# Mixture logits: the bias in the place of the last feature

## The chip, the cores and the metric

The kernel runs on one core of a Trainium2 chip. The metric is the time of one execution on the device in microseconds; a run gives one time, and the median of several is compared. Engines are named as in the profile: PE is TensorE (PEld its weight loads), DVE is VectorE, ACT is ScalarE, POOL is GpSimd, and SP is SyncE, which here only issues DMA transfers.

## The reference

4,096 tokens of 256 features pass through attention, a mixture layer, a second attention and the same mixture layer again, each on the layer-normed input and added to it. This is the mixture layer (n = 64 experts of p = 32 slots, 2,048 slots in all):

```python
logits = (jnp.einsum('tzd,ed->tze', x, phi_w) + phi_b).reshape(t, z, n, p)
D = jax.nn.softmax(logits, axis=3)
C = jax.nn.softmax(logits, axis=2)
X_tilde = jnp.einsum('tznp,tzd->npd', D, x)
...
X_tilde = jnp.tanh(X_tilde)
Y_tilde = jnp.einsum('npd,ndH->npH', X_tilde, expert_w) + expert_b[:, None, :]
Y = jnp.einsum('tznp,npH->tzH', C, Y_tilde)
```

The `x` of this function is a layer norm without weights: the 256 features of a token have mean zero, so the last one is minus the sum of the others.

## The kernel before

The program is a row of stages, one after the other, with a barrier of all engines between them (`phase_of`). Each engine has its instruction list for a stage, and semaphores order them inside it. The stages are: `load_and_cut`; then for each of the two halves (tags a and f, then b and g) a layer norm, the projections, attention and output projection, and for the mixture layer (f, g) a layer norm, `dispatch`, `experts` and `combine`.

**load_and_cut** (DVE, POOL, SP, a little PE; the first 43 us). SP loads phi transposed, two groups of 128 features by 2,048 slots. DVE finds the largest magnitude (a maximum and a minimum over everything, L96 and L97, then a transpose on PE to spread it over partitions), and cuts phi, scaled by a power of two, into a high and a low half of 16 bits (L123, L125), which SP stores in DRAM as `phi_parts` for both mixture layers. It does the same for the bias row, on one partition, in three bf16 parts (L221 to L229, `bparts`), stored as `pb_parts`. DVE's last work there is the scales of the attention weights (L217, L219, a gather on PE at L200, L233 to L245). POOL builds identity matrices and masks from tiles that DVE clears; SP copies two of them with their halves swapped (`mask_turned`, `identb_turned`) at the end of its list, behind the store of `pb_parts`.

**The layer norm of a mixture layer** writes the normed tokens scaled by 256, transposed (features on partitions), as a high and a low half: `xlnT[feature, part, c, token]`. While it runs, SP loads its list `loads`: phi's two parts, the bias parts `pb3`, and `pbcol`, the bias with slots on partitions.

**dispatch** works in 64 units: 32 tiles of 128 tokens for the first 1,024 slots, and the same for the others. For unit n, PE computes the logits into two PSUM banks: for each bank six matmuls (high x high, high x low, low x high, for two groups of features; L1002) and one with the bias (L1004), 3 rows of ones against the three bias parts. DVE takes the maxima over the slots of an expert (L1105) and over the experts (L1106, kept for combine), and subtracts the first (L1110). ACT exponentiates (L1042); DVE sums (L1094) and inverts (L1098), ACT scales the inverse (L1047), POOL multiplies (L1083), ACT casts to the high half (L1050), POOL makes the low half (L1087), and PE multiplies with the tokens, 24 matmuls into four accumulator banks (L1015). The lists are staggered:

```python
for n in range(UNITS_D + LAG):
    if n < UNITS_D:
        logits(n)
    if n >= LAG:
        products(n - LAG)
    if n in TURN_AFTER:
        turn(TURN_AFTER[n])
```

`LAG` is 3. On DVE, the sum and inverse of unit n-1 stand behind the subtraction of unit n; on ACT the exponential of n stands ahead of the scaling and the cast of n-1. The logits have two slots of two banks, so `logits(n)` waits for the subtraction of n-2. After 8 units of the second half (n = 39, 47, 55, 63) a chunk of maxima is combined on DVE (L1117) and cut in three by four small operations on POOL, between the multiplication and the low half of that unit; three units later PE transposes it (L1024) in one of the logits slots, and ACT copies it out behind its cast of that iteration. When the first half is through, ACT copies the four accumulators out (L1055), and the products of unit 32 wait for it.

**combine** computes the logits again, transposed, 16 blocks for each group of 512 tokens, with six matmuls (L1268) and one (L1272) that subtracts the kept maxima; the bias comes in as ACT's per-partition operand of the exponential (L1319).

Of the kernel before, what the change touches and what calls it, by code (L numbers as in the profile page):

```python
# [129 lines left out]
def load_and_cut(nc, m, ps, x_in, phi_in, pb_in, phi_parts, pb_parts, qk_weights):  # L130
# [3 lines left out]
    with phase_of(nc, "cut") as (ctx, sem, sb):  # L134
        phi, parts = sb("phi", [P, DC, SLOTS]), sb("parts", [P, 2, DC, SLOTS], F16)
        row, rest = sb("row", [1, SLOTS]), sb("rest", [1, SLOTS])
        bparts = sb("bparts", [1, 3, SLOTS], BF16)
# [66 lines left out]
        def _(dve):  # L204
# [19 lines left out]
            dve.wait_ge(row_cut, 2)  # L224
            dve.tensor_tensor(rest[:, :], row[:, :], bparts[:, 0, :], ALU.subtract).then_inc(row_cut, 1)
            dve.wait_ge(row_cut, 3)
            dve.tensor_copy(bparts[:, 1, :], rest[:, :]).then_inc(row_cut, 1)
# [1258 lines left out]
```

## Time and profile before

| | |
|---|---|
| median of 3 runs | 5185.71 us |
| lowest, highest | 5184.31, 5189.25 us |
| the profiled execution | 5181.14 us |
| its span, first to last instruction | 5179.4 us |
| mean granted clock of TensorE | 0.944 of full |
| PE busy | 4608.4 us (89%) |
| DVE busy | 4098.5 us (79%) |
| ACT busy | 3144.7 us (61%) |
| POOL busy | 1188.4 us (23%) |
| first dispatch stage, first to last matmul | 1688.5 to about 2104 us |
| second dispatch stage, first matmul | 4253.8 us |

The profile is of one execution, and its rows are times within that. Busy shares are means over stages with different limits; what an edit is worth is read from its own stage. A full clock is 1.00, which is 2.4 GHz; 0.50 is 1.2 GHz.

### The profile page before, as it was taken

To read this page: it belongs to the slowest core of one execution; us is meant where nothing else is said; L and a number is where in the kernel's file an instruction comes from. 1 tells how busy PE (TensorE), PEld (TensorE's weight loads), DVE (VectorE), ACT (ScalarE), POOL (GpSimd) and SP (SyncE) were. 2 spreads that over 40 slices of the span, in tenths; PEclk is the share of its full clock that TensorE was granted. 3 is DMA by queue.
4 is the path that set the end of the run, shared out by engine and by line. 5 is a ranking of instruction groups with operands and counts; after the bars stand their busy time and mean duration, and the time that the engine had idled before them with its cause. 6 is when DMAs were issued, how large, how long until landed. Compare 5 with 4: busy or idle time off the path is not lost. (4 is left out here: it accounts for less than half of the span.)

```text
span 5179.4 us, 97856 instructions
## 1 busy us (share of the span) xinstructions
PE 4608.4 (89%) x40558; PEld 2002.5 (39%) x40558; DVE 4098.5 (79%) x4682; ACT 3144.7 (61%) x5855; POOL 1188.4 (23%) x1174
## 2 busy tenths in 40 slices
PE   5589999999997999689867899999999979996998
PEld 2322223322234555355533222232222345552555
DVE  5399999999875778477745999999998768774776
ACT  1267898889995334234323789888899933332433
POOL 0000001100003567243300000011000126662342
PEclk9699999999998999799977999999999989997999
DMA  3100000000000000400021000000000000005000
GB/s 125 47 20 8 2 14 14 14 14 2 2 2 21 1 1 1 147 1 0 1 68 34 17 8 2 19 9 14 14 2 2 2 19 1 1 1 147 9 12 13
DMA packets 70480, 106.94 MB, mean 21 GB/s; under 512 B 9465, under 2 KB 57721, under 8 KB 65919
## 3 DMA queue, kind: packets, MB, share of 16 engines
q1 hardware_dynamic: 70064, 101.08, 6.1%
q8 instruction: 300, 4.92, 0.4%
q14 instruction: 116, 0.94, 0.1%
HBM read 76.73 MB, written 23.08 MB: 19 GB/s over the span
## 5 line engine op out<-in xcount | busy, mean ns | idle before, releaser
L871 DVE TENSOR_REDUCE b_att_mx<-ps 128x2 f32<-128x1024 f32 (+3 forms) x1152 | 1227.3, 1130 | 112.4 <-PE ps L724 71.6
L871 DVE TENSOR_REDUCE a_att_mx<-ps 128x2 f32<-128x1024 f32 (+3 forms) x1152 | 1227.3, 1130 | 110.7 <-PE ps L724 69.7
L828 ACT ACTIVATE a_att_pt<-ps 128x512 f32<-128x512 f32 (+3 forms) x2304 | 1149.5, 561 | 212.7 <-PE ps L760 180.6
L828 ACT ACTIVATE b_att_pt<-ps 128x512 f32<-128x512 f32 (+3 forms) x2304 | 1149.7, 561 | 211.3 <-PE ps L760 179.6
L779 PE MATMUL ps<-b_att_pt,b_v 128*17 128x256 f32 (+1 forms) x8704 | 671.3, 381 | 9.7 <-ACT b_att_osb L815 9.0
L779 PE MATMUL ps<-a_att_pt,a_v 128*17 128x256 f32 (+1 forms) x8704 | 671.2, 381 | 9.7 <-ACT a_att_osb L815 9.1
L760 PE MATMUL ps<-b_q,b_k 51*128 51x512 f16 (+3 forms) x1152 | 367.0, 369 | 0.3 <-ACT b_att_pt L828 0.2
L760 PE MATMUL ps<-a_q,a_k 51*128 51x512 f16 (+3 forms) x1152 | 366.9, 369 | 0.3 <-ACT a_att_pt L828 0.2
L760 PE MATMUL ps<-a_att_q,a_att_k 51*128 51x512 f16 (+3 forms) x1152 | 340.4, 365 | 1.0 <-ACT a_att_pt L828 0.7
L760 PE MATMUL ps<-b_att_q,b_att_k 51*128 51x512 f16 (+3 forms) x1152 | 339.9, 365 | 1.3 <-ACT b_att_pt L828 0.5
L705 POOL TENSOR_SCALAR_AFFINE_SELECT b_att_pt<-b_att_pt 128x512 f32<-128x512 f32 x128 | 81.4, 636 | 1126.8 <-ACT b_att_pt L828 1114.4
L705 POOL TENSOR_SCALAR_AFFINE_SELECT a_att_pt<-a_att_pt 128x512 f32<-128x512 f32 x128 | 81.3, 636 | 1125.8 <-ACT a_att_pt L828 1113.4
L724 PE MATMUL ps<-a_k,a_q 48*128 48x512 f16 (+3 forms) x1152 | 290.2, 380 | 36.3 <-DVE a_att_mx L871 32.8
L724 PE MATMUL ps<-b_att_k,b_att_q 48*128 48x512 f16 (+3 forms) x1152 | 318.7, 365 | 3.0 <-DVE b_att_mx L871 2.5
L724 PE MATMUL ps<-a_att_k,a_att_q 48*128 48x512 f16 (+3 forms) x1152 | 317.9, 365 | 3.0 <-DVE a_att_mx L871 2.5
L724 PE MATMUL ps<-b_k,b_q 48*128 48x512 f16 (+3 forms) x1152 | 289.5, 379 | 34.1 <-DVE b_att_mx L871 30.5
L779 PEld LDWEIGHTS ps<-a_att_pt,a_v 128*17 128x17 f32 x8704 | 145.5, 95 | 358.0 <-ACT a_att_pt L828 217.5
L779 PEld LDWEIGHTS ps<-b_att_pt,b_v 128*17 128x17 f32 x8704 | 145.6, 96 | 357.2 <-ACT b_att_pt L828 212.5
L1319 ACT ACTIVATE g_comb_ct<-ps,g_pbcol,unscale 128x512 f32<-128x512 f32 x128 | 99.3, 776 | 208.4 <-PE ps L1272 208.4
L1319 ACT ACTIVATE f_comb_ct<-ps,f_pbcol,unscale 128x512 f32<-128x512 f32 x128 | 99.3, 776 | 207.5 <-PE ps L1272 207.5
L1281 PE MATMUL ps<-f_comb_yp,f_comb_ct 128*128 128x256 f16 x1536 | 186.2, 282 | 38.2 <-DVE f_comb_ct L1366 38.2
L1281 PE MATMUL ps<-g_comb_yp,g_comb_ct 128*128 128x256 f16 x1536 | 186.3, 282 | 37.0 <-DVE g_comb_ct L1366 37.0
(309 smaller groups left out, 7652.5 us busy)
## 6 DMA issues: line engine op xcount, KB each, us to landing
f_exp_w<-in_expert_w SPq DMA_DIRECT2D x64, 256.0 KB, 5.8
g_exp_w<-in_expert_w SPq DMA_DIRECT2D x64, 256.0 KB, 5.4
x<-in_x SPq DMA_DIRECT2D x1, 4096.0 KB, 19.6
a_parts_q<-a_qkv_cut SPq DMA_DIRECT2D x16, 256.0 KB, 2.8
a_parts_k<-a_qkv_cut SPq DMA_DIRECT2D x16, 256.0 KB, 2.7
b_parts_q<-b_qkv_cut SPq DMA_DIRECT2D x16, 256.0 KB, 2.8
b_parts_k<-b_qkv_cut SPq DMA_DIRECT2D x16, 256.0 KB, 2.7
out<-x SPq DMA_DIRECT2D x8, 512.0 KB
```

The lines of the kernel that those rows point to most:

```text
L705: pool.affine_select(out=block_p, in_=block_p, pattern=[[0, 4], [1, P]], compare_op=ALU.is_ge, fill=0.0, base=0, channel_multiplier=-1).th ...
L724: mm = pe.matmul(ps[:, at:at + width], q[quad % 2][h // 2][r:r + ROWS, t0:t0 + P], k[quad % 2][h // 2][r:r + ROWS, c * BANK:c * BANK + wid ...
L760: pe.matmul(ps[:, at:at + width], k[quad % 2][h // 2][r:r + ROWS_M, kb * P:(kb + 1) * P], q[quad % 2][h // 2][r:r + ROWS_M, (g + 1) * BANK ...
L779: mm = pe.matmul(OUT[32 * h:32 * h + VW, lo:hi], v[:, kb, 4 * quad + h, :], pt[:, s % PT_RING, h, lo - left:hi - left], start=(first and h ...
L828: act.activation(pt[:, s % PT_RING, i, 0:width], ps[:, at:at + width], ACT.Exp, scale=unscale).then_inc(pt_ready, 1)
L871: dve.tensor_reduce(mx[u % 2][:, h:h + 2, t, c], both, AX.X, ALU.max).then_inc(ring_read, 1)
L1281: mm = pe.matmul(ps[:, (Y + zt) * BANK:(Y + zt) * BANK + D], ctp[1 - parity][:, kb, cp * BANK + zt * P:cp * BANK + (zt + 1) * P], yp[:, y, ...
L1319: act.activation(ct[parity][:, b, :], ps[:, (LT + b % 4) * BANK:(LT + b % 4 + 1) * BANK], ACT.Exp, bias=pbcol[:, b:b + 1], scale=m.unscale ...
```

## The change

The layer-normed features add up to zero, so a sum over 256 features with weights w is a sum over the first 255 with weights w minus the last weight. The place of the 256th is free: its row of phi holds the bias, divided by 2^15 / 256, and its row of `xlnT` the constant 2^15. The logits come out of the six matmuls with the bias in them; the bias matmul of dispatch, the bias parts and the bias operand of combine are gone. The subtraction is done once, on the chip, in `load_and_cut`.

```diff
@@ load_and_cut
-        row, rest = sb("row", [1, SLOTS]), sb("rest", [1, SLOTS])
-        bparts = sb("bparts", [1, 3, SLOTS], BF16)
+        last, col = sb("last", [P, SLOTS]), sb("col", [P, 1])
+        ones_row = sb("ones_row", [1, 2, N], F16)
...
-            sp.dma_start(row[:, :], pb_in.rearrange("(a s) -> a s", a=1)).then_inc(row_loaded, 16)
+            sp.dma_start(last[:, :], last_in.partition_broadcast(P)).then_inc(loaded, 16)
...
-            sp.wait_ge(row_cut, 6)
-            sp.dma_start(pb_parts, bparts[:, :, :]).then_inc(stored, 16)
-            sp.wait_ge(built, 1)
+            sp.wait_ge(row_made, 2)
+            sp.dma_start(x_rows, ones_row[:, :, :]).then_inc(stored, 16)
+            sp.wait_ge(built, 2)
...
+            pool.memset(ones_row[:, 0, :], X_ONE).then_inc(row_made, 1)
+            pool.memset(ones_row[:, 1, :], 0.0).then_inc(row_made, 1)
             pool.wait_ge(cleared, 1)
+            pool.affine_select(out=col[:, :], in_=col[:, :], pattern=[[0, 1]], compare_op=ALU.not_equal,
+                               fill=XLN_SCALE / X_ONE, base=1 - P, channel_multiplier=1).then_inc(built, 1)
+            pool.wait_ge(built, 1)
...
-            dve.memset(m.onesb[:, :], 1.0).then_inc(cleared, 1)
-            dve.wait_ge(loaded, 16)
+            dve.memset(col[:, :], 1.0).then_inc(cleared, 1)
+            dve.wait_ge(loaded, 32)
+            dve.tensor_tensor(phi[:, 0, :], phi[:, 0, :], last[:, :], ALU.subtract).then_inc(folded, 1)
+            dve.tensor_tensor(phi[0:P - 1, 1, :], phi[0:P - 1, 1, :], last[0:P - 1, :], ALU.subtract).then_inc(folded, 1)
+            dve.wait_ge(built, 1)
+            dve.wait_ge(folded, 2)
+            dve.tensor_scalar(phi[P - 32:P, 1, :], phi[P - 32:P, 1, :], col[P - 32:P, 0:1], None, ALU.mult).then_inc(folded, 1)
+            dve.wait_ge(folded, 3)
             n = scales.make(dve, phi_f, ps[:, 0:P], chain, gathered)
...
-            dve.wait_ge(row_loaded, 16)
-            dve.tensor_scalar(row[:, :], row[:, :], bscale[0:1, 0:1], None, ALU.mult).then_inc(row_cut, 1)
-            dve.wait_ge(row_cut, 1)
-            dve.tensor_copy(bparts[:, 0, :], row[:, :]).then_inc(row_cut, 1)
...
-            dve.tensor_tensor(bparts[:, 2, :], rest[:, :], bparts[:, 1, :], ALU.subtract).then_inc(row_cut, 2)
-            dve.wait_ge(row_cut, 6)
@@ layernorm
-            return xlnT[:, part, c, tg * BANK:(tg + 1) * BANK], ps[:, (i % 4) * BANK:(i % 4 + 1) * BANK]
+            rows = P - (c == DC - 1)
+            return xlnT[0:rows, part, c, tg * BANK:(tg + 1) * BANK], ps[0:rows, (i % 4) * BANK:(i % 4 + 1) * BANK]
@@ dispatch, logits(n)
-                        pe.matmul(ps[:, at:at + BANK], xlnT[:, xp, c, t * P:(t + 1) * P], phi[:, pp, c, e0:e0 + BANK],
-                                  start=(i == 0), stop=False)
-                    mm = pe.matmul(ps[:, at:at + BANK], m.onesb[0:3, :], pb3[0:3, e0:e0 + BANK], start=False, stop=True)
+                        mm = pe.matmul(ps[:, at:at + BANK], xlnT[:, xp, c, t * P:(t + 1) * P], phi[:, pp, c, e0:e0 + BANK],
+                                       start=(i == 0), stop=(i == len(TERMS) - 1))
@@ combine
-                                       bias=pbcol[:, b:b + 1], scale=m.unscale[:, 0:1]).then_inc(ct_exp, 1)
+                                       scale=m.unscale[:, 0:1]).then_inc(ct_exp, 1)
@@ mixture_layer
-                loads += [(pb3[0:3, :], pb_parts.rearrange("a i s -> (a i) s")), (pbcol[:, :], t["phi_bT"])]
+                loads += [(xlnT[P - 1:P, :, DC - 1, :], x_rows)]
@@ kernel
-    arrays["phi_wT"] = _np.asarray(inputs["L0_ffn_phi_w"]).T
-    arrays["phi_b"] = inputs["L0_ffn_phi_b"]
-    arrays["phi_bT"] = _np.asarray(inputs["L0_ffn_phi_b"]).reshape(EB, P).T
+    phi_wT = _np.asarray(inputs["L0_ffn_phi_w"]).T
+    arrays["phi_wT"] = _np.concatenate([phi_wT[:D - 1], _np.asarray(inputs["L0_ffn_phi_b"])[None]])
+    arrays["phi_last"] = phi_wT[D - 1]
```

Three places as the engines' lists show them. On PE, where dispatch of layer f takes up its products (`f_phi` and `f_xlnT` are the logits' operands, `f_pb` the bias parts, `f_xtok` the tokens), before:

```order
L1004 MATMUL ps<-f_pb,onesb 128x512
L1002 MATMUL ps<-f_phi,f_xlnT 128x512 x6
L1004 MATMUL ps<-f_pb,onesb 128x512
L1015 MATMUL ps<-f_xtok,f_disp_disp 128x256 x24
L1002 MATMUL ps<-f_phi,f_xlnT 128x512 x6
L1004 MATMUL ps<-f_pb,onesb 128x512
L1002 MATMUL ps<-f_phi,f_xlnT 128x512 x6
L1004 MATMUL ps<-f_pb,onesb 128x512
L1015 MATMUL ps<-f_xtok,f_disp_disp 128x256 x24
```

and now:

```order
L1002 MATMUL ps<-f_phi,f_xlnT 128x512 x48
L1014 MATMUL ps<-f_xtok,f_disp_disp 128x256 x24
L1002 MATMUL ps<-f_phi,f_xlnT 128x512 x12
L1014 MATMUL ps<-f_xtok,f_disp_disp 128x256 x24
L1002 MATMUL ps<-f_phi,f_xlnT 128x512 x12
```

Nothing stands between the twelve logits matmuls of a unit; the products keep their place.

On DVE, at the start of `load_and_cut`, before:

```order
L208 MEMSET onesb 128x128
L96 TENSOR_REDUCE cut_phi_top<-cut_phi 128x1
L97 TENSOR_REDUCE cut_phi_bottom<-cut_phi 128x1
L99 SCALAR_TENSOR_TENSOR cut_phi_largest<-cut_phi_bottom,cut_phi_top 128x1
L101 COPY cut_phi_spread<-cut_phi_largest 128x128
```

and now (`cut_last` is the last feature's weights on every partition, `cut_col` a column of ones with the bias factor on the last partition):

```order
L214 MEMSET cut_col 128x1
L216 TENSOR_TENSOR cut_phi<-cut_phi,cut_last 128x2048
L217 TENSOR_TENSOR cut_phi<-cut_phi,cut_last 127x2048
L220 TENSOR_SCALAR cut_phi<-cut_phi,cut_col 32x2048
L97 TENSOR_REDUCE cut_phi_top<-cut_phi 128x1
L98 TENSOR_REDUCE cut_phi_bottom<-cut_phi 128x1
```

Three operations over 2,048 elements have moved ahead of the reductions.

On DVE again, behind the cutting of phi, before:

```order
L125 SCALAR_TENSOR_TENSOR cut_parts<-cut_phi,cut_phi_scale,cut_parts 128x4096
L217 TENSOR_REDUCE cut_wtop<-cut_wqk 128x4
L219 COPY cut_wspread<-cut_wtop 128x512
L221 TENSOR_SCALAR cut_row<-cut_row,cut_bscale 1x2048
L223 CAST cut_bparts<-cut_row 1x2048
L225 TENSOR_TENSOR cut_rest<-cut_row,cut_bparts 1x2048
L227 CAST cut_bparts<-cut_rest 1x2048
L229 TENSOR_TENSOR cut_bparts<-cut_rest,cut_bparts 1x2048
L233 TENSOR_REDUCE cut_wtop<-ps 128x4
```

and now:

```order
L126 SCALAR_TENSOR_TENSOR cut_parts<-cut_phi,cut_phi_scale,cut_parts 128x4096
L228 TENSOR_REDUCE cut_wtop<-cut_wqk 128x4
L230 COPY cut_wspread<-cut_wtop 128x512
L232 TENSOR_REDUCE cut_wtop<-ps 128x4
L234 TENSOR_SCALAR cut_wtop<-cut_wtop 128x4
```

The five operations on the bias row are gone from between the spread of the weights' maxima and the reduction of what PE gathered.

## Rows read from the trace of the kernel before

**Rows 1.** Stretches: us; busy (count) of PE, PEld, DVE, ACT, POOL; clock; DMA; GB/s

```profile
1717.68:2082.84 365.16, 361.14 (x2267) 210.73 (x2267) 296.50 (x298) 146.27 (x183) 242.32 (x130) 1.00 0.00 1
...
1905.44:1916.22 10.78, 7.81 (x39) 4.52 (x40) 4.96 (x5) 5.20 (x8) 7.36 (x4) 0.84 0.01 2
1934.39:1983.88 49.49, 49.15 (x313) 28.75 (x313) 40.91 (x42) 20.27 (x25) 34.32 (x21) 1.00 0.00 1
```

**Rows 2.** Timeline of one unit of the first dispatch stage: start us, us, engine

```profile
1850.82 2.79 PE L1015 MATMUL ps<-f_xtok,f_disp_disp 128*128 128x256 f16 x24
1850.93 1.23 DVE L1105 TENSOR_REDUCE f_disp_md<-ps 128x32 f32<-128x1024 f32 x1 [1.06 <-PE ps L1004]
...
1853.20 1.22 DVE L1110 TENSOR_TENSOR f_disp_shifted<-ps,f_disp_md 128x1024 f32<-128x1024 f32 x1
...
1853.45 1.46 PE L1002 MATMUL ps<-f_phi,f_xlnT 128*128 128x512 f16 x6
...
1855.16 1.47 PE L1002 MATMUL ps<-f_phi,f_xlnT 128*128 128x512 f16 x6
...
1856.27 1.91 POOL L1083 TENSOR_TENSOR f_disp_ex<-f_disp_ex,f_disp_rds 128x1024 f32<-128x1024 f32 x1 [0.80 <-ACT f_disp_rds L1047]
1856.56 0.09 PEld L1004 LDWEIGHTS ps<-f_pb,onesb 3*128 3x128 bf16 x1 [0.42 <-issue]
1856.56 0.39 PE L1004 MATMUL ps<-f_pb,onesb 3*128 3x512 bf16 x1
...
1856.88 2.79 PE L1015 MATMUL ps<-f_xtok,f_disp_disp 128*128 128x256 f16 x24
...
1858.27 1.04 ACT L1050 CAST f_disp_disp<-f_disp_ex 128x1024 f16<-128x1024 f32 x1 [2.07 <-POOL f_disp_ex L1083]
...
1859.39 2.13 POOL L1087 TENSOR_TENSOR f_disp_disp<-f_disp_ex,f_disp_disp 128x1024 f16<-128x1024 f32 x1 [1.21 <-ACT f_disp_disp L1050]
```

**Rows 3.** Timeline of the second combine stage: two blocks of logits on TensorE

```profile
4748.77 1.46 PE L1268 MATMUL ps<-g_xlnT,g_phi 128*128 128x512 f16 x6
...
4750.29 1.46 PE L1268 MATMUL ps<-g_xlnT,g_phi 128*128 128x512 f16 x6
```

**Rows 4.** Timeline at the switch to the second half, TensorE

```profile
1908.41 1.90 PE L1015 MATMUL ps<-f_xtok,f_disp_disp 128*128 128x256 f16 x11 [3.00 <-ACT f_xacc L1055]
```

**Rows 5.** Timeline where a chunk of maxima is cut: VectorE, GpSimd, TensorE

```profile
1937.80 1.41 DVE L1117 TENSOR_TENSOR f_disp_mc<-f_disp_mcp 128x256 f32<-128x256 f32 x1
...
1946.27 1.92 POOL L1083 TENSOR_TENSOR f_disp_ex<-f_disp_ex,f_disp_rds 128x1024 f32<-128x1024 f32 x1
...
1950.56 2.13 POOL L1087 TENSOR_TENSOR f_disp_disp<-f_disp_ex,f_disp_disp 128x1024 f16<-128x1024 f32 x1
...
1952.74 2.79 PE L1015 MATMUL ps<-f_xtok,f_disp_disp 128*128 128x256 f16 x24 [0.22 <-POOL f_disp_disp L1087]
```

**Rows 6.** Timeline of the start-up stage and the start of what follows

```profile
8.89 4.42 DVE L96 TENSOR_REDUCE cut_phi_top<-cut_phi 128x1 f32<-128x4096 f32 x1 [7.25 <-DMA cut_phi<-in_phi_wT]
...
29.84 2.08 PE L200 MATMUL ps<-ident,cut_wspread 128*128 128x128 f32 x8 [10.83 <-DVE cut_wspread L219]
...
32.26 2.28 DVE L225 TENSOR_TENSOR cut_rest<-cut_row,cut_bparts 1x2048 f32<-1x2048 f32 x1
...
38.21 0.69 DVE L233 TENSOR_REDUCE cut_wtop<-ps 128x4 f32<-128x512 f32 x1
...
39.68 0.16 DVE L245 TENSOR_SCALAR qk_unscale<-qk_unscale 128x2 f32<-128x2 f32 x1
...
43.08 1.41 DVE L315 BATCH_NORM_STATS2 a_ln_stats<-x 128x6 f32<-128x256 f32 x4 [3.24 <-PEq L75]
```

**Rows 7.** Line 481: count, duration min/median/max ns, first and last start

```profile
L481 POOL MEMSET a_qkv_minus<- x1: 3501/3501/3501, 76.6 to 76.6; 3x4096 f16 x1
```

**Rows 8.** Groups by line: the exponentials of the first combine stage

```profile
L1319 ACT ACTIVATE f_comb_ct<-ps,f_pbcol,unscale 128x512 f32<-128x512 f32 x128 | 99.3, 776 | 207.5 <-PE ps L1272 207.5
```

**Rows 9.** Timeline at the end of the first dispatch stage, TensorE

```profile
2094.80 5.30 PE L1015 MATMUL ps<-f_xtok,f_disp_disp 128*128 128x256 f16 x24 [4.58 <-POOL f_disp_disp L1087]
```

More of the change, by code:

```diff
@@ L51 @@
 XLN_SCALE = 256.0
+X_ONE = 2.0 ** 15
 D_SCALE = 2.0 ** 14
@@ L126, in cut, with load_and_cut @@
                                  ALU.mult, ALU.subtract).then_inc(done, 1)
-def load_and_cut(nc, m, ps, x_in, phi_in, pb_in, phi_parts, pb_parts, qk_weights):
+def load_and_cut(nc, m, ps, x_in, phi_in, last_in, phi_parts, x_rows, qk_weights):
     with phase_of(nc, "cut") as (ctx, sem, sb):
         phi, parts = sb("phi", [P, DC, SLOTS]), sb("parts", [P, 2, DC, SLOTS], F16)
-        row, rest = sb("row", [1, SLOTS]), sb("rest", [1, SLOTS])
-        bparts = sb("bparts", [1, 3, SLOTS], BF16)
-        scales, bscale = Scales(sb, "phi"), sb("bscale", [P, 1])
-        loaded, row_loaded, x_loaded = sem("loaded"), sem("row_loaded"), sem("x_loaded")
+        last, col = sb("last", [P, SLOTS]), sb("col", [P, 1])
+        ones_row = sb("ones_row", [1, 2, N], F16)
+        scales = Scales(sb, "phi")
+        loaded, x_loaded = sem("loaded"), sem("x_loaded")
+        folded, row_made = sem("folded"), sem("row_made")
         cleared, built = sem("cleared"), sem("built")
@@ L144, in load_and_cut @@
         phi_cut = sem("phi_cut")
-        row_cut = sem("row_cut")
         stored = sem("stored")
@@ L212, in _ @@
             dve.tensor_scalar(scales.scale[:, :], scales.inverse[:, :], TOP, None, ALU.mult).then_inc(chain, 1)
-            dve.tensor_scalar(bscale[:, :], scales.inverse[:, :], TOP * XLN_SCALE, None, ALU.mult).then_inc(chain, 1)
-            dve.wait_ge(chain, n + 3)
+            dve.wait_ge(chain, n + 2)
             scales.cut(dve, phi_f, parts_f, phi_cut)
@@ L219, in _ @@
             dve.tensor_copy(wspread[:, :, :], wtop[:, :].unsqueeze(2).broadcast_to([P, 4, P])).then_inc(w_chain, 1)
-            dve.wait_ge(row_loaded, 16)
-            dve.tensor_scalar(row[:, :], row[:, :], bscale[0:1, 0:1], None, ALU.mult).then_inc(row_cut, 1)
-            dve.wait_ge(row_cut, 1)
-            dve.tensor_copy(bparts[:, 0, :], row[:, :]).then_inc(row_cut, 1)
[L224 to L227, printed above, removed]
-            dve.wait_ge(row_cut, 4)
-            dve.tensor_tensor(bparts[:, 2, :], rest[:, :], bparts[:, 1, :], ALU.subtract).then_inc(row_cut, 2)
-            dve.wait_ge(row_cut, 6)
             dve.wait_ge(w_gathered, 1)
@@ L929, in _, with dispatch @@
                                   ALU.add).then_inc(added, 1)
-def dispatch(nc, m, ps, tag, xtok, xlnT, phi, pb3, xacc, mct):
+def dispatch(nc, m, ps, tag, xtok, xlnT, phi, xacc, mct):
     UNIT = SLOTS // 2
@@ L1207, in _, with combine @@
                 mm.then_inc(y_ready, 1)
-def combine(nc, m, ps, tag, xlnT, phi, pbcol, mct, yt, out):
+def combine(nc, m, ps, tag, xlnT, phi, mct, yt, out):
     AHEAD = 10
@@ L1445, in mixture_layer @@
                         layernorm(nc, m, ps, f"{tag}_ln", xln, xlnT, xtok, loads)
-                    dispatch(nc, m, ps, f"{tag}_disp", xtok, xlnT, phi, pb3, xacc, mct)
+                    dispatch(nc, m, ps, f"{tag}_disp", xtok, xlnT, phi, xacc, mct)
                 experts(nc, m, ps, f"{tag}_exp", xacc, xacc, t["expert_w"], t["expert_b"])
-                combine(nc, m, ps, f"{tag}_comb", xlnT, phi, pbcol, mct, xacc, out if last else None)
+                combine(nc, m, ps, f"{tag}_comb", xlnT, phi, mct, xacc, out if last else None)
         attention_layer("a", 0, t["a_WqT"], t["a_WkT"], t["a_WvT"], t["a_WoT"], t["a_bo"], t["a_db"])
```

12 lines of the change are left out of this document (5 added, 7 removed).

## The prediction

> **What bounds the kernel now.** Begin with the table of stretches. The change touches a start-up stage of 43 us, the two layer norms of the mixture layers, their two dispatch stages (some 415 us each) and one operand in the combine stages; the attention halves keep every instruction. In the body of the first dispatch stage TensorE is busy for 361 of 365 us at the full clock, VectorE for 297 and GpSimd for 242 [rows 1]; the second repeats it. So TensorE bounds them as they stand. Next, one unit on the timeline: the logits of 128 tokens by 1,024 slots. Its pattern repeats every 6.055 us: the products of unit n-3 (L1015) start at 1850.82 and the next ones at 1856.88, and VectorE's first reduction (L1105) starts 0.11 behind them, having idled 1.06 for TensorE [rows 2]. I call that start S(n). From the fifth unit's S at 1717.68 to the 64th's at 2082.84 there are 59 periods, which make 357.2 of the 365.16 us [rows 1]. The other 8 are a stall at the half switch (10.78 instead of 6.06, so 4.7) and 1.04 for each of three chunks of maxima (49.49 for eight units, against 48.45) [rows 1].
>
> **What the bias products cost.** Two of them leave each unit, 128 each layer. Take the half with 1855.16: six logits matmuls start there, the bias matmul at 1856.56, and what follows it at 1856.88, which is 1.72 us for seven [rows 2]. In combine, six of these matmuls and one with 96 rows go from 4748.77 to 4750.29, 1.52 for seven, 0.216 each, with a change of bank after each seven and no gap [rows 3]. So six cost 1.30, and the bias one is worth 0.42: 0.216 for its columns and 0.2 because its weight load was not done ahead (PEld shows 0.42 us idle in front of it and begins as late as the matmul [rows 2]). I take 0.42, as measured in the stage itself. TensorE's own unit becomes 2.63 (24 products, 1850.82 to 1853.45 [rows 2]) + 12 x 0.216 = 5.22 us.
>
> The Trainium skill, "TensorE: Matmul & The Clock Gate", section "Back-to-back issue gap", gives a 512-column matmul 512/2.4 + 2.5 = 216 ns whatever its rows; by that the pair would be worth 0.43 a unit and not 0.84. The trace agrees with 216 ns for the full matmuls and disagrees for the one with 3 rows.
>
> **What is late next.** 0.84 does not come back whole, because a loop closes first. Follow S = 1850.93: the reduce, the maxima, the subtraction at 1853.20, then the sum and reciprocal of the unit before and ScalarE's scaling, until GpSimd multiplies at 1856.27 (S + 5.34), ScalarE casts at 1858.27 and GpSimd subtracts from 1859.39 to 1861.52 (S + 10.59) [rows 2]. These are the products' operands for unit n-1. TensorE asks for them at S + 2 x 6.055 - 0.11 = 12.0, so they have 1.4 us of slack. With T = 5.22, TensorE would want them at S + 2T - 0.1 = 10.34, before they exist. So the order is: operands at 10.59, products at 10.64, next logits 2.63 later, ready 2.59 + 0.11 after that: S(n+3) = S(n) + 15.97, T = 5.32. GpSimd with ScalarE between its halves needs 3.12 + 2.13 = 5.25 at most [rows 2], VectorE 5.0 (6.06 less its idle 1.06). All three fit under 5.32, but barely. Saving per unit 6.055 - 5.32 = 0.735; times 59 = 43.4 us a layer.
>
> The loop has no slack, so what was absorbed is now paid. A chunk of maxima: VectorE's extra operation is 1.41 [rows 5], which delays GpSimd's multiply by 1.33; in the next unit four small cuts make multiply-to-subtract 4.29 instead of 3.12 [rows 5]. Counted through: operands of that unit +2.4. Then TensorE transposes (0.7), and the logits after next wait until ScalarE, which casts first, has emptied the slot (0.6). In all about 3.6 instead of 1.04, three times: 7.7 back. Half switch: products of unit 32 waited 3.00 us for ScalarE's copies of the accumulators [rows 4], which sit behind its cast; TensorE comes there 0.7 sooner, so the wait grows by 0.7. Start: two bias products of the first unit, still at 1.2 GHz, and two of the fifth lie ahead of the fifth unit's S: some 0.9 each pair, 1.8 gained. The drain after the last S is GpSimd's chain and keeps its length. Layer: 43.4 - 7.7 - 0.7 + 1.8 = 36.8. Both: 73.6.
>
> **The start-up stage.** VectorE now waits also for a broadcast row, 1 MB. 2 MB were there at 8.89 [rows 6], so 1 MB is 2.6 if the rate of the body holds, and 4 at most. Then two subtractions at 2.28 (the row with 2,048 elements [rows 6]) and a scaling for which I take half of that: 2.6 + 4.6 + 1.3 = 8.5 later. The five one-partition operations between the weights' reduction and L233 go. TensorE's gather, which ends at 31.92 (29.84 + 2.08 [rows 6]), was hidden by them; it ends at 40.4 now, so L233 starts at 40.6 instead of 38.21, and VectorE ends at 42.2 (39.84 + 2.4). The layer norm began at 43.08 [rows 6], after the turned masks' transfers, which were issued behind L229. These now leave at 36, once the second part of phi is cut, and land by 41 to 42. So the stage keeps its end: 0, with -0.5 and +3 as bounds (a late broadcast, a slow row). GpSimd's two memsets come first in its stream, 3.50 each at most by the row with three partitions [rows 7]; its masks then end near 13, before VectorE's reductions ask TensorE for anything.
>
> **Edits at nothing.** In the layer norms, one partition less changes no length, and three loads instead of four land within a stage of 40 us; uncovered, they would be some 3 us a layer. The exp in combine loses its bias pointer. Ahead of it ScalarE idles 207 us for TensorE [rows 8] and may get shorter than 776 ns; its cover is TensorE's 1.52 a block. Gone or not, GpSimd could start 0.2 sooner at 16 group starts: 0 to 3 us, taken as 0.
>
> **Sum.** 5181.1 (the profiled execution, span 5179.4) - 73.6 = 5107.5. That execution is 4.6 under the median of the three runs, so the median comes out at 5185.7 - 73.6 = **5112**.
>
> **The rivals.**
> - A, the loop (0.62): 5112, own range 5099 to 5124 (T by 0.04 either way is 5, chunks and switch 6, the clock at the starts 5).
> - B, the loop does not bite (0.10), since GpSimd or VectorE hand over earlier than I added up: T = 5.22, chunks and switch as before, 59 x 0.835 + 1.8 = 51.1 a layer, 5083.5. Against it: the hand-overs are the same to 0.01 in each unit of the trace.
> - C, the bias product is worth its columns alone (0.10): the 0.2 of gap belongs to something that stays, as the bank change. T = 5.62, under the loop's reach, 59 x 0.43 + 1 a layer, 5133. That is the skill's rule above. Against it: combine changes banks without a gap [rows 3].
> - D, engines that no longer rest slow each other (0.12): VectorE's sum and GpSimd's subtraction read the same memory at once. With 0.18 a unit, T = 5.5, 59 x 0.555 - 6.6 = 26 a layer, 5133. Against more than that: GpSimd is at work through most of each unit already [rows 2].
> - E, slower (0.03): TensorE now waits some 0.1 in every unit. After 4.58 us idle it ran 24 products in 5.30, at 1.2 GHz, instead of 2.79 [rows 2, 9]. Should the granted clock fall inside the loop, a unit takes 10.4. At 14 such units of 118 the gain is gone (73.6 / 5.1); with a third of them the time is 5312. Against it: at the chunk it waited 0.22 us and kept its 2.79 [rows 5], and it stays 98% busy.
> - F, nothing moves (0.03): the start-up grows by what dispatch gives back. It would need 60 us more there; I see 4.
>
> **How the numbers follow.** A measurement tells about 0.2% (10 us) from no change. A to D are faster: 0.94. F is the same: 0.03. E is slower: 0.03. The range takes in C and D and most of the way to B: 5091 to 5135.
>
> **What would show it.** In the changed profile S to S should be 5.3 us in the body (5.22 B, 5.62 C, 5.5 D), with VectorE's idle before L1105 near 0.3 to 0.5 and a wait of about 0.1 us of TensorE for GpSimd's subtraction before each group of products; twelve logits matmuls in 2.6 us; eight units with a chunk at 45 to 46 us; dispatch clock 1.00; the first layer norm's start within 3 us of 43.1; the exp of combine shorter and its stages within 3 us of before. It is wrong if the twelve matmuls keep gaps, or if GpSimd's or VectorE's operations have grown.

## The result, and the profile after

| | before | changed |
|---|---|---|
| median | 5186.89 us (with the runs shown ahead) | 5122.96 us, 4 runs |
| lowest, highest | 5184.31, 5189.25 us | 5120.71, 5127.49 us |
| ratio, 95% interval | 1 | 0.9881, 0.9867 to 0.9894 |
| profiled execution, its span | 5181.14, 5179.4 us | 5120.71, 5119.0 us |

The change is 63.9 us faster by the medians, where 74 were predicted (5112); the time lies in the range. A second set of the changed kernel gives 5121.77. S is, as in the prediction, the start of VectorE's first reduction of a unit. First the windows of the first dispatch stage: the fifth unit's S to the 64th's, the half switch, and eight units with the second chunk in them; columns as in [rows 1].

```profile
1724.62:2060.45 335.83, 318.92 (x2150) 208.19 (x2149) 297.28 (x298) 145.97 (x184) 241.85 (x130) 0.98 0.00 1
1890.58:1902.24 11.66, 7.87 (x38) 4.89 (x39) 4.96 (x5) 5.23 (x9) 8.08 (x4) 0.71 0.00 0
1965.07:2012.76 47.69, 44.49 (x298) 29.11 (x297) 41.15 (x41) 20.18 (x25) 34.23 (x21) 0.96 0.00 1
```

Fifty-nine periods take 335.83 us instead of 365.16 [rows 1], 29.3 less, where 35.0 were predicted (43.4 - 7.7 - 0.7). The switch takes 11.66 instead of 10.78, eight units with a chunk 47.69 instead of 49.49. The granted clock is 0.98 over the stretch (1.00 before), 0.71 at the switch (0.84 before) and 0.96 in the eight units (1.00 before).

The same stretch of the second dispatch stage, before and changed:

```profile
4279.23:4645.61 366.38, 362.35 (x2267) 211.32 (x2267) 296.52 (x298) 147.32 (x184) 243.99 (x131) 0.99 0.00 1
...
4257.20:4589.66 332.46, 314.86 (x2150) 206.14 (x2149) 297.30 (x299) 145.84 (x183) 241.71 (x130) 0.99 0.00 1
```

There it is 33.9 less. The second stage does not repeat the first, before or after: its half switch took 12.01 us before and takes 8.91 now.

Next the timeline of one unit, to be laid beside [rows 2].

```profile
1831.51 1.22 DVE L1104 TENSOR_REDUCE f_disp_md<-ps 128x32 f32<-128x1024 f32 x1 [0.22 <-PE ps L1002]
...
1831.71 2.79 PE L1014 MATMUL ps<-f_xtok,f_disp_disp 128*128 128x256 f16 x24 [0.24 <-POOL f_disp_disp L1086]
...
1833.63 1.04 ACT L1049 CAST f_disp_disp<-f_disp_ex 128x1024 f16<-128x1024 f32 x1 [2.08 <-POOL f_disp_ex L1082]
...
1834.34 2.75 PE L1002 MATMUL ps<-f_phi,f_xlnT 128*128 128x512 f16 x12
1834.75 2.14 POOL L1086 TENSOR_TENSOR f_disp_disp<-f_disp_ex,f_disp_disp 128x1024 f16<-128x1024 f32 x1 [1.21 <-ACT f_disp_disp L1049]
...
1836.94 2.79 PE L1014 MATMUL ps<-f_xtok,f_disp_disp 128*128 128x256 f16 x24
1837.13 1.23 DVE L1104 TENSOR_REDUCE f_disp_md<-ps 128x32 f32<-128x1024 f32 x1 [0.62 <-PE ps L1002]
```

VectorE's first reduction starts at 1831.51 and 1837.13. The reader is to see who waits: TensorE 0.24 us for GpSimd's low half at 1831.71, and nothing at 1836.94, where the low half was done only 0.05 us earlier (1834.75 + 2.14). In the body the starts repeat 5.22, 5.22, 5.63: from 1821.05 to 1837.13 three units take 16.08. Their mean is 5.36. The twelve logits matmuls begin at 1834.34 and the products after them at 1836.94, 2.60 us, which is 12 x 0.216.

TensorE at the half switch and around the second chunk, to be laid beside [rows 4, 5]:

```profile
1894.37 5.24 PE L1014 MATMUL ps<-f_xtok,f_disp_disp 128*128 128x256 f16 x24 [3.83 <-ACT f_xacc L1054]
...
1930.70 2.79 PE L1014 MATMUL ps<-f_xtok,f_disp_disp 128*128 128x256 f16 x24 [2.00 <-POOL f_disp_disp L1086]
...
1977.45 4.46 PE L1014 MATMUL ps<-f_xtok,f_disp_disp 128*128 128x256 f16 x24 [2.00 <-POOL f_disp_disp L1086]
1981.75 2.75 PE L1002 MATMUL ps<-f_phi,f_xlnT 128*128 128x512 f16 x12
1984.34 2.78 PE L1014 MATMUL ps<-f_xtok,f_disp_disp 128*128 128x256 f16 x24
1986.96 0.61 PE L1023 MATMUL ps<-identb,f_disp_m 128*96 128x128 bf16 x8
1988.08 2.76 PE L1002 MATMUL ps<-f_phi,f_xlnT 128*128 128x512 f16 x12 [0.51 <-DVE f_disp_shifted L1109]
...
1993.88 2.76 PE L1002 MATMUL ps<-f_phi,f_xlnT 128*128 128x512 f16 x12 [0.42 <-ACT f_mct L1060]
```

The wait for the accumulators' copies is 3.83 instead of 3.00, and the products behind it take 5.24. At each chunk TensorE now waits 2.00 for GpSimd, where it waited 0.22. Behind the first of these waits (1930.70) the 24 products keep their 2.79; behind the second (1977.45) and the third they take 4.46. At the second chunk 0.51 and 0.42 follow, for VectorE's subtraction and for ScalarE's copy out of the slot.

In the second dispatch stage TensorE waits about as long at the half switch, but there it is the changed kernel whose products keep the full clock. The first row is the kernel before, the second the changed one:

```profile
4469.95 5.28 PE L1015 MATMUL ps<-g_xtok,g_disp_disp 128*128 128x256 f16 x24 [3.00 <-ACT g_xacc L1055]
...
4426.97 2.78 PE L1014 MATMUL ps<-g_xtok,g_disp_disp 128*128 128x256 f16 x24 [3.54 <-ACT g_xacc L1054]
```

The start-up stage, beside [rows 6]:

```profile
11.40 2.29 DVE L216 TENSOR_TENSOR cut_phi<-cut_phi,cut_last 128x2048 f32<-128x2048 f32 x1 [9.88 <-DMA cut_last<-in_phi_last]
...
17.43 4.42 DVE L97 TENSOR_REDUCE cut_phi_top<-cut_phi 128x1 f32<-128x4096 f32 x1
...
38.32 2.08 PE L206 MATMUL ps<-ident,cut_wspread 128*128 128x128 f32 x8 [10.77 <-DVE cut_wspread L230]
...
40.44 0.69 DVE L232 TENSOR_REDUCE cut_wtop<-ps 128x4 f32<-128x512 f32 x1 [2.17 <-PE ps L206]
...
43.03 1.41 DVE L315 BATCH_NORM_STATS2 a_ln_stats<-x 128x6 f32<-128x256 f32 x4 [0.96 <-PEq L76]
```

The broadcast was there at 11.40, the reductions begin at 17.43 instead of 8.89, the gathered maxima are reduced at 40.44 instead of 38.21, and the layer norm begins at 43.03, where it began at 43.08. VectorE idled 3.24 us ahead of it and now idles 0.96.

The exponentials of the first combine stage, beside [rows 8]:

```profile
L1318 ACT ACTIVATE f_comb_ct<-ps,unscale 128x512 f32<-128x512 f32 x128 | 87.7, 685 | 213.8 <-PE ps L1271 213.8
```

They last 685 ns instead of 776, and ScalarE's idle time before them has grown from 207.5 to 213.8 us. The Trainium skill, "ScalarE: Activation LUTs", section "What ACT_TABLE_LOAD costs", says that each operand given as a pointer to one value a partition adds about 93 ns to such an instruction; the rows agree, with 91.

### The profile page after: what moved, and what is told of

It is laid out like the page before. It is cut to its first block and busy times, and to the rows that moved or that the text cites. A ratio compares the mean times of both kernels' runs of the same rounds, so it can differ in the third digit from the quotient of the medians.

```text
span 5119.0 us, 97342 instructions
## 1 busy us (share of the span) xinstructions
PE 4521.4 (88%) x40302; PEld 1996.8 (39%) x40302; DVE 4094.9 (80%) x4679; ACT 3125.4 (61%) x5855; POOL 1204.5 (24%) x1177
## 5 line engine op out<-in xcount | busy, mean ns | idle before, releaser
L1318 ACT ACTIVATE g_comb_ct<-ps,unscale 128x512 f32<-128x512 f32 x128 | 87.7, 685 | 213.9 <-PE ps L1271 213.9
L1318 ACT ACTIVATE f_comb_ct<-ps,unscale 128x512 f32<-128x512 f32 x128 | 87.7, 685 | 213.8 <-PE ps L1271 213.8
```

The costliest lines, as they stand in the source:

```text
L1318: act.activation(ct[parity][:, b, :], ps[:, (LT + b % 4) * BANK:(LT + b % 4 + 1) * BANK], ACT.Exp, scale=m.unscale[:, 0:1]).then_inc(ct_ex ...
```

## Experiments

Times are medians. The runs of before that went with e1 to e4 have a median of 5185.84 us, those of e5 to e8 5184.0, and those of e9 to e11 5184.8. e4, e7, e9 and e10 are one execution each, and single executions of one kernel differ by some 10 us. Where a gain is smaller than that, a layer's own rows tell more: from the layer norm's first transposition on TensorE to the experts' first product the mixture layers take 477.6 and 476.9 us before, 445.8 and 442.8 in the changed kernel, and 445.8 and 442.8 again in its second profile (e8).

### The matmul alone, or its gap alone (e1, e2)

```diff
- mm = pe.matmul(..., m.onesb[0:3, :], pb3[0:3, e0:e0 + BANK], ...)   # before
+ mm = pe.matmul(..., m.onesb[:, :], pb3[:, e0:e0 + BANK], ...)       # e1; pb3 has 128 rows, cleared once a layer
```

> The kernel before, with its bias matmul given 128 rows instead of 3 (ones against the three bias parts and 125 rows of zeros, which a small stage of its own clears once for each layer, some 3 us each). Theory, the gap of 0.2 us belongs to the 3-row form: the matmul costs 0.216 us instead of 0.42, the unit is 5.22 + 2 x 0.216 = 5.65 us, above the loop's 5.36, so 59 x 0.405 = 24 us less a layer and 48 less in all, minus 6 for the clearing: about 5145. Rival, the gap comes from the bias matmul's place (last of an accumulation, bf16 behind f16, before a change of bank): the unit stays at 6.06 us and the time at 5187 to 5193.

Measured: 5151.58 us (5146.76 to 5154.17), ratio 0.9935 [0.9919, 0.9952]. The timeline of the logits in dispatch:

```profile
1852.71 1.46 PE L1002 MATMUL ps<-f_phi,f_xlnT 128*128 128x512 f16 x6
...
1853.79 0.10 PEld L1004 LDWEIGHTS ps<-f_pb,onesb 128*128 128x128 bf16 x1
...
1854.00 0.38 PE L1004 MATMUL ps<-f_pb,onesb 128*128 128x512 bf16 x1
1854.00 1.18 PEld L1002 LDWEIGHTS ps<-f_phi,f_xlnT 128*128 128x128 f16 x6
1854.22 1.46 PE L1002 MATMUL ps<-f_phi,f_xlnT 128*128 128x512 f16 x6
```

The weight load of the bias matmul (PEld) begins 0.21 ahead of its matmul, and the next six follow 0.22 behind it. Before, the load began together with the matmul, and what follows came 0.32 later [rows 2]. The unit is 5.64 us, so 0.415 of each 6.055 was the gap of two matmuls with three rows, and not a property of the place. The median lies 7 us above what I expected: 59 x 0.415 is 24.5 a layer, but less slack makes the chunks dearer here already, which is 11 us in both layers (eight units with one take 48.07, 2.9 above 8 x 5.64, against 1.04 before).

> The kernel before with nothing changed but that the bias matmul of dispatch is left out (the logits of dispatch lack the bias; the start-up stage, the layer norms and combine are those of before). Theory, the whole gain is made by this matmul's absence: the unit is 5.357 us as in the changed kernel, its dispatch stages as long, and the time within 4 us of the changed kernel's (5123), up to 4 above it for the combine stages. Rival, the start-up stage or the loads of the changed kernel cost something (the attention of the first half took 8 us longer in its profile): this kernel would be some 8 us faster than the changed one, at 5115.

```diff
-                        pe.matmul(..., start=(i == 0), stop=False)
-                    mm = pe.matmul(ps[:, at:at + BANK], m.onesb[0:3, :], pb3[0:3, e0:e0 + BANK], start=False, stop=True)
+                        mm = pe.matmul(..., start=(i == 0), stop=(i == len(TERMS) - 1))
```

Measured: 5120.91 us (5116.68 to 5125.05), ratio 0.9877 [0.9861, 0.9894]. TensorE in the body:

```profile
1853.48 2.75 PE L1002 MATMUL ps<-f_phi,f_xlnT 128*128 128x512 f16 x12
1856.48 2.79 PE L1014 MATMUL ps<-f_xtok,f_disp_disp 128*128 128x256 f16 x24 [0.24 <-POOL f_disp_disp L1086]
```

This is the changed kernel's pattern, 0.24 of waiting every third unit included, and the same time within 2 us; the layers take 446.0 and 443.3 us. So the matmul is the whole gain, and everything else in the change (start-up, rows of the layer norm, loads, the operand of combine) is worth nothing that a measurement can tell.

### How many rows the gap needs (e9, e10)

The edits are that of e1 with 32 and with 96 rows.

> The kernel before with 32 rows in the bias matmul instead of 3 (the 29 others hold zeros, cleared once for each layer; the logits are the same). With 128 rows the bias matmul cost 0.216 us, its columns, and its weight load was done ahead; with 3 rows it cost 0.42. Two theories of the gap. If it belongs to a weight load that fills less than a full row of tiles of the array (3 of 32 rows, as against whole groups of 32), 32 rows already take the gap away: the unit of dispatch is 5.64 us as with 128 rows, and the time near 5152. If any weight load that uses far fewer rows than its neighbours keeps the gap, the unit is 6.05 us as before, and the time near 5186 to 5190 (the clearing adds some us). I hold the second likelier (0.6), since nothing in the rows distinguishes 3 from 32 but their number.

> The kernel before with 96 rows in the bias matmul. In combine a matmul with 96 rows between others with 128 shows no gap, and its weight load is done ahead. If what counts is the number of rows, the unit of dispatch is 5.64 us here as with 128 rows and the time near 5152 (0.9). If the gap belonged to something else in dispatch that 128 rows alone cure, the unit stays 6.05 and the time near 5188.

Measured: 5183.28 us with 32 rows (the second theory, held at 0.6) and 5152.01 with 96 (as expected). With 32 rows the weight load still begins with its matmul, 0.42 us after the load before it, and the next load waits 0.23:

```profile
1853.82 0.09 PEld L1004 LDWEIGHTS ps<-f_pb,onesb 32*128 32x128 bf16 x1 [0.42 <-issue]
1853.83 0.39 PE L1004 MATMUL ps<-f_pb,onesb 32*128 32x512 bf16 x1
1854.14 2.52 PEld L1015 LDWEIGHTS ps<-f_xtok,f_disp_disp 128*128 128x128 f16 x24 [0.23 <-issue]
```

With 96 rows it is ahead, and nothing waits:

```profile
1855.61 0.10 PEld L1004 LDWEIGHTS ps<-f_pb,onesb 96*128 96x128 bf16 x1
...
1855.82 0.38 PE L1004 MATMUL ps<-f_pb,onesb 96*128 96x512 bf16 x1
1855.83 1.18 PEld L1002 LDWEIGHTS ps<-f_phi,f_xlnT 128*128 128x128 f16 x6
```

A matmul of 512 columns between ones with 128 rows costs 0.42 us with 3 or 32 rows and 0.216 with 96 or 128. Where it turns between 32 and 96, and why, no run here shows.

### The loop through the lag (e4, e3, e11)

```diff
-    LAG, EX, DISP = 3, 4, 3
+    LAG, EX, DISP = 2, 4, 3      # e4, in the changed kernel
+    LAG, EX, DISP = 4, 4, 3      # e3 in the changed kernel, e11 in the one before
```

> The changed kernel with LAG = 2. Theory of the loop: the same 16.07 us are shared by two units, 8.03 each, so 59 x 2.68 = 158 us more a layer, 5123 + 316 = about 5440, more if the clock falls while TensorE waits 2.8 us in every unit (a unit then has up to 2.6 + 2.6 us more in the loop, 10.6, and the time would be 5740). Rival, the unit is bound by an engine's own work (TensorE 5.22, GpSimd 5.2): it stays near 5.4 and the time near 5125.

Measured: 5539.21 us. TensorE in the body, and the window of the stage:

```profile
1851.95 5.30 PE L1014 MATMUL ps<-f_xtok,f_disp_disp 128*128 128x256 f16 x24 [5.47 <-POOL f_disp_disp L1086]
1857.05 3.22 PE L1002 MATMUL ps<-f_phi,f_xlnT 128*128 128x512 f16 x12
...
1717.00:2290.00 573.00, 390.38 (x2244) 248.23 (x2242) 307.90 (x319) 157.89 (x198) 257.39 (x140) 0.84 0.01 2
```

TensorE waits 5.47 us for GpSimd in every second unit, and what follows runs at the lower clock in part: 24 products in 5.30 (4.78 in the next pair) and twelve logits matmuls in 3.22. The granted clock of the stage is 0.84. In the first half of the stage two units take 17.6 to 19.0; the pair shown takes 19.0, of which (5.30 - 2.79) + (3.22 - 2.75) = 3.0 are the clock. Without it they take 16.0: the loop, as it was counted, now closes over two units instead of three. So the time comes out between the two that were expected, because the clock falls in part of the loop.

> The changed kernel with the products of dispatch four units behind the logits instead of three (LAG = 4). Theory, a loop of 16.07 us over LAG units bounds the unit: at LAG = 4 it allows 4.02, so TensorE bounds it at 5.22, TensorE no longer waits before the products, the chunks of maxima no longer stop it for 2 us and its clock no longer falls there; 59 x 0.137 = 8 us a layer for the loop, 3 x 3 = 9 for the chunks: 34 in all, about 5089. Rival D, engines that never rest slow each other or GpSimd is the bound: the unit stays at 5.36 and the time at 5123.

Measured: 5103.98 us (5102.61 to 5104.29), ratio 0.9842 [0.9826, 0.9859]. In the body (from the 16th unit; the ones before come every 4.85, while TensorE works off the room of the longer lag) every unit takes 5.21, TensorE's own time, with no wait for GpSimd. That is what the loop predicts for a fourth unit of room. But the time is 15 above what was expected, and TensorE shows where, at the half switch and at the third chunk of the first stage:

```profile
1883.46 5.28 PE L1014 MATMUL ps<-f_xtok,f_disp_disp 128*128 128x256 f16 x24 [8.22 <-ACT f_xacc L1054]
...
2017.19 2.76 PE L1002 MATMUL ps<-f_phi,f_xlnT 128*128 128x512 f16 x12 [1.62 <-DVE f_disp_shifted L1109]
...
2025.24 4.45 PE L1002 MATMUL ps<-f_phi,f_xlnT 128*128 128x512 f16 x12 [2.66 <-ACT f_mct L1060]
```

The products of unit 32 wait 8.22 for the accumulators' copies and run at the lower clock (5.28). At the chunk 2.66 goes to ScalarE's copy of the maxima out of a logits slot, and the logits behind it take 4.45 instead of 2.75; at the second chunk, behind the same 2.66, they take 2.76. Both copies stand behind a cast, and the cast behind GpSimd: what the lag gave in the body, ScalarE's order took back in part. The layers take 440.0 and 437.1 us, 11.5 less in both than in the changed kernel; the rest of the 19 by the medians lies outside them.

> The kernel before, with its bias matmul, and LAG 4 instead of 3. Theory: before the change TensorE's own unit (6.055 us) was longer than the loop asks for, so the products' operands had 1.4 us of slack, and a lag of 4 gives nothing in the body: unit 6.05 us. It takes away the waits before the first products, and moves the chunks and the half switch as it did in the changed kernel (a longer wait for the accumulators' copies). Time 5180 to 5190, ratio 0.999 to 1.001. Rival: the lag is worth the same 19 us here as in the changed kernel (5122 to 5104), which would mean that it acts at the starts and chunks and not through the loop: 5167.

Measured: 5168.68 us (5163.78 to 5172.6, 7 runs), ratio 0.9968 [0.9957, 0.998]. The forecast was wrong, and the rival's number came. The body is as I expected, 6.055 a unit, so the loop gave nothing. The gain is in the run-up (to the eighth unit's S) and in the drain, 8.5 us in the first layer and 7.2 in the second, which I had not counted; the half switch took 1.1 back in the first and gave 1.2 in the second. TensorE, where the first products are taken up and at the half switch:

```profile
1704.88 1.47 PE L1002 MATMUL ps<-f_phi,f_xlnT 128*128 128x512 f16 x6 [1.34 <-DVE f_disp_shifted L1110]
...
1708.32 2.79 PE L1015 MATMUL ps<-f_xtok,f_disp_disp 128*128 128x256 f16 x24
...
1905.20 5.28 PE L1015 MATMUL ps<-f_xtok,f_disp_disp 128*128 128x256 f16 x24 [3.00 <-ACT f_xacc L1055]
```

The first products run at 1708.32 without a wait and in 2.79; with a lag of three they waited 3.54 us and then took 5.30 in the first layer (2.79 in the second, behind the same wait). From the first transposition of the layer norm to the experts' first product, the first layer is 7.3 us shorter and the second 8.4. So e3's 19 us can't stand as proof of the loop: from the first S to the fifth alone e3 gains 4.0 us a layer, and e11 gains 5.0 and 2.1 there. The proof is the unit, 5.36 to 5.21 with the lag in the changed kernel, and 6.055 to 6.055 in the one before.

### ScalarE's copies ahead of its cast (e5, e6)

```diff
                     act.activation(rds[:, v % 2, :], rd[:, v % 2, :], ACT.Copy, scale=D_SCALE).then_inc(r_scaled, 1)
-                    wait(act, xa_ready, v - DISP + 1)
-                    act.wait_ge(d_made, v + 1)
-                    act.copy(disp[:, v % DISP, 0, :], ex[:, v % EX, :]).then_inc(high, 1)
                 if n - LAG in (T - 1, UNITS_D - 1):
...
+                if 0 <= v < UNITS_D:
+                    wait(act, xa_ready, v - DISP + 1)
+                    act.wait_ge(d_made, v + 1)
+                    act.copy(disp[:, v % DISP, 0, :], ex[:, v % EX, :]).then_inc(high, 1)
```

> The changed kernel with ScalarE's two kinds of copies in dispatch (the accumulators at the half switch, the turned maxima) put between its scaling and its cast of an iteration, where it idles 2 us for GpSimd, instead of behind the cast. Theory: the wait of 3.8 us for the accumulators shrinks to some 0.6 and, with so short a stop, TensorE's clock does not fall there (products took 5.24 instead of 2.79), 5.3 us a layer; the wait for the turned maxima (0.42) goes in each chunk, 1.5 a layer; the loop keeps the unit at 5.36. 14 us in all: about 5108. Rival, the copies delay the cast and so the loop: no gain, 5121 or more.

Measured: 5109.78 us (5108.96 to 5111.47), ratio 0.9852 [0.9836, 0.9869], near the 5108 expected. TensorE at the half switch, and at a chunk:

```profile
1883.22 2.78 PE L1014 MATMUL ps<-f_xtok,f_disp_disp 128*128 128x256 f16 x24 [0.69 <-ACT f_xacc L1051]
...
1964.64 4.46 PE L1014 MATMUL ps<-f_xtok,f_disp_disp 128*128 128x256 f16 x24 [2.00 <-POOL f_disp_disp L1087]
```

The wait for the copies is 0.69 instead of 3.83, and the products keep 2.78. The chunk is hardly changed: 2.00 for GpSimd and 4.46 of products are still there, since VectorE's and GpSimd's extra work makes the operands late and no copy does. The match with 5108 is in part luck: the layers take 440.8 and 440.8 us, 5.0 and 2.0 less than in the changed kernel, 7 in all where 14 were expected. The 5.3 and the 1.5 a layer were counted from the first stage and for both; in the second stage the changed kernel's clock had not fallen at the switch, and the chunks got no cheaper (47.1 to 47.5 for eight units in both stages, against 46.8 to 47.7). The rest of the 12 by the medians lies where the edit changes nothing.

> Both: LAG = 4 and ScalarE's copies between its scaling and its cast. Theory: with LAG = 4 TensorE waited 8.2 us at the half switch and 2.7 at the turned maxima in each chunk for copies that stood behind casts, and its clock fell after both; these go, so a layer gains 10 + 3 x 3 = 19 over LAG = 4 alone (5104), 38 in all: about 5066. Rival, the stops at the chunks are those for the slot of logits, for VectorE's subtraction, and stay: 5104 - 20 = 5084.

Measured: 5074.74 us (5068.18 to 5083.57, 4 runs), ratio 0.9781 [0.9765, 0.9797]: 48 us under the changed kernel, the fastest kernel here, and between the 5066 expected and the rival's 5084. TensorE at the half switch and at the first chunk:

```profile
1885.72 4.05 PE L1014 MATMUL ps<-f_xtok,f_disp_disp 128*128 128x256 f16 x24 [2.45 <-ACT f_xacc L1051]
...
1923.50 2.76 PE L1002 MATMUL ps<-f_phi,f_xlnT 128*128 128x512 f16 x12 [1.62 <-DVE f_disp_shifted L1110]
```

In the first stage the switch costs a wait of 2.45 and a piece of the clock (4.05), in the second 4.47 and 5.28. The first chunk costs the 1.62 shown and no fall of the clock; the second and third have no wait above 0.52, and eight units with one of them take 42.8, against 47.7. The two edits are worth 19 and 13 us alone and 48 together by the medians, and 11.5, 7 and 44.9 by the rows of the layers (420.8 and 422.9 here): a lag of four removes what makes the operands late, and the moved copies what the longer lag would have put in its place.

### The rest of the change, and the spread (e7, e8)

```diff
                         act.activation(ct[parity][:, b, :], ps[:, (LT + b % 4) * BANK:(LT + b % 4 + 1) * BANK], ACT.Exp,
-                                       bias=pbcol[:, b:b + 1], scale=m.unscale[:, 0:1]).then_inc(ct_exp, 1)
+                                       scale=m.unscale[:, 0:1]).then_inc(ct_exp, 1)
```

> The kernel before with nothing changed but that the exponential of combine has no bias operand (combine's logits lack the bias). Theory: the exponential is 0.09 us shorter (687 instead of 776 ns), hidden by TensorE; the combine stages keep their 379 us within 2, and the time stays at 5186 within 5. Rival: the shorter exponentials gave the changed kernel the 1 and 2.5 us by which its combine stages were shorter; they show here too, 376 to 377.

Measured: 5187.46 us, against 5184.0. Two rows of this kernel's profile, the first transpositions of mixture layer f (count, duration, first and last start) and its exponentials:

```profile
L265 PE MATMUL ps<-ident,f_xln x64: 421/421/477, 1658.6 to 1694.9; 128*128 128x128 f32 x64
...
L1319 ACT ACTIVATE f_comb_ct<-ps,unscale 128x512 f32<-128x512 f32 x128 | 87.8, 686 | 215.5 <-PE ps L1272 215.5
```

The exponentials are 90 ns shorter, as in the changed kernel, and the time has not moved: TensorE covers them. The combine stages take 377.1 us each, which is the rival's number and not the 379 expected; but in e8, which has no bias operand either, they take 379.5 and 379.6, so one execution of e7 doesn't speak for the rival.

> The changed kernel again, on this chip. Theory: the 8 us by which the first attention stage was longer in its profile are the clock of that one execution; the stage takes 1357 to 1360 us here, the time is about 5121. Rival: the stage is slower whenever this kernel runs: 1365, and 5123 or more.

Measured: 5121.77 us (5113.09 to 5128.37), ratio 0.9873 [0.9856, 0.9889]. The first attention stage takes 1362.9 us, between the 1360 of the theory and the 1365 of the rival. What speaks against the rival is e7: its attention is that of the kernel before, and it takes 1365.2, where the profile before has 1357.6 and the changed one 1365.3.

The spread of single executions has one place that can be named. In the profiled execution of the changed kernel those transpositions began late:

```profile
L264 PE MATMUL ps<-ident,f_xln x64: 421/421/476, 1659.5 to 1695.8; 128*128 128x128 f32 x64
```

They begin at 1659.5 there and at 1658.6 in e7, whose attention and everything ahead of it is that of the kernel before; in the profile before they start at 1649.7, and in e11 at 1648.0. So some 9 to 10 us come or go ahead of the mixture layer in kernels of both kinds, and this comparison of two executions happens to hold it against the change. The granted clock goes with them: from 240 to 1000 us it is 0.98 in the profile before and 0.99 in e11, but 0.96 in the changed kernel's and 0.97 in e7 and e8.

## Why the prediction was right, and what was off

**What bounds it, and the matmul's price: right.** TensorE's own unit went from 6.055 to 5.21, the predicted 5.22, and e2 has the whole gain in one edit. Half of the price is the gap of matmuls with three rows; e1 gets 0.415 of the 0.84 back with more rows. Rival C falls with that: the twelve logits matmuls of the changed kernel follow each other without a gap. The rule of the Trainium skill weighed there ("TensorE: Matmul & The Clock Gate", section "Back-to-back issue gap") gives 216 ns, by a formula in which the rows don't occur and which the Trainium skill gives there for the gap of an isolated matmul; for a stream of loads and matmuls the same section has about 131 ns. The traces measure 216 ns in the stream for 96 and 128 rows, and 0.42 us for 3 and 32.

**The loop: right, its period 0.04 too short.** Three units take 16.08, and 15.97 were predicted. The chain itself was met: in the unit above the low half is done at 1834.75 + 2.14 = 1836.89, S + 10.61 for the S at 1826.28 (predicted 10.59). Nearly all the rest is the 0.11 that I put between the products' start and VectorE's. It is 0.19 now (1836.94 to 1837.13). Before, the products themselves started 0.32 behind the last logits matmul, because of the gap; now they start 0.22 behind it, and VectorE waits for the end of that matmul all the same. A loss of 59 x 0.037, 2.2 us a layer. Rival B falls with it, and D too: at 16.08 for three units with the durations as before, no engine slows another (GpSimd's low half is 2.14 and was 2.13).

**The chunks and the half switch: the step that was mis-sized.** "In all about 3.6 instead of 1.04, three times" came out, in the first stage, as 3.9, 4.8 and 4.8 (46.76, 47.69 and 47.69 for eight units, less 8 x 5.357 = 42.9), and the switch as 6.3 where 5.4 were predicted. I counted the waits and not what the clock may do behind them. The first chunk shows the waits alone: the clock holds, and it costs 3.9, 0.3 above the count. In the second and third the products take 4.46 instead of 2.79 behind the same 2.00; that is 1.7 more, of which 0.9 reach the period, since the waits that follow get shorter. Behind the 3.83 they take 5.24, 0.8 more than the 4.45 of all 24 behind the 3.00 of before, whose first eleven are in [rows 4]. This is a piece of rival E, priced there for the loop alone. e5 shortens the wait at the switch to 0.69 and has the 2.78 back. But the length of a wait doesn't settle it: in the second stage the first two chunks cost 3.9 and only the third 4.8, and the switch 3.6, because its products keep 2.78 behind 3.54 us. Two of the signs named for the trace failed with this step: eight units with a chunk were to take 45 to 46 us, and the clock of dispatch was to be 1.00.

**Where the 10 us went.** The prediction priced the first layer and doubled it, 36.8 each. The two layers gain 31.7 and 34.1 us, 65.8 for 73.6 predicted, and not in the same places:

| a layer's gain, us | predicted | first | second |
|---|---|---|---|
| first transposition to the fifth unit's S | 1.8 | 2.8 | -1.3 |
| fifth unit's S to the 64th's | 35.0 | 29.3 | 33.9 |
| 64th unit's S to the experts' first product | 0 | -0.4 | 1.5 |

In the middle row the first layer lacks 5.7 us: 2.2 by the period, 2.8 by the chunks, 0.9 by the switch (5.9 by these rounded terms). The second lacks 1.1, since its switch was dearer before (12.01) and is cheaper now (8.91). Its start is dearer: before, the products there waited 3.54 us and took 2.79; now they wait 4.28 and take 5.30. That the sum comes within 8 us of the prediction is in part luck, as the unpriced clock went for the change in one place and against it in another. The combine stages are 1.1 and 2.5 shorter, but in e5 and e8, which have no bias operand either, they take 379.3 to 379.6 (378.4 and 379.8 before), so that is their spread. The 9 to 10 us ahead of the first mixture layer are spread too. The two profiled executions so differ by 60.4, the medians by 63.9.

**The start-up stage: right.** 8.5 later in VectorE's chain was 8.54, the reduction that was L233 was forecast at 40.6 and came at 40.44 (now L232), VectorE ends at 42.07, and the layer norm starts 0.05 sooner than before. The added subtractions and the scaling were paid out of the five one-partition operations that are gone and of VectorE's idle time at the end of the stage (3.24 us before, 0.96 now). Rival F is out.

**Open.** What makes TensorE's clock fall behind one wait and not behind another of the same length, which is where the two layers differ; and what makes it differ ahead of the first mixture layer from one execution to the next.

## What to carry to other kernels

A matmul with few rows among full ones can cost twice its columns, as it did here, where its weight load was not done ahead: count such matmuls by the distance to what follows, not by their own bar. When the bounding engine gets shorter, follow the loop through the other engines over as many units as the lag has, and price each stall that its slack used to absorb, with the clock that may fall behind it: here between 0 and 2.5 us for 24 products, so it belongs in the range and not in the sum. Check the second layer's rows too, before you double the first's. And when a longer lag disappoints, look for work of an old unit that sits in an engine's list behind a wait of a newer one.

## What the hardware showed that was not expected

- The weight load for 3 or 32 rows between loads for 128 began with its matmul (0.42 us idle ahead of it, 0.23 ahead of the next); for 96 and 128 rows it began 0.21 ahead. The cost is 0.2 us for each such matmul, and the clock has no part in it, since TensorE was at full clock in all four.
- 24 products take 2.79 us at 2.4 GHz and 5.30 at 1.2 GHz (granted clock 1.00 and 0.50), so a stop can cost up to 2.5 us above its length. Its length alone doesn't tell whether it does. Behind a wait of 2.00 us they took 2.79 in three chunks of the changed kernel's profile and 4.46 in the other three. Behind 3.54 us they took 5.30 in the first stage before and 2.79 in the second, and 2.78 at the second switch of the changed kernel. Behind 3.00 us they took 4.45 and 5.28 before, 5.28 and 4.05 in e11. Behind 0.22 to 0.69 us they took 2.78 or 2.79 in every row shown.
- A pointer operand less on ScalarE's exponential over 512 columns: 91 ns.
